# A four-layer residual kernel: the gated layer's first tokens and first weights prepared in the last two attention bodies, and output weights awaited where they are used

## What is computed

```python
x = x + L0(x)      # 16-head attention with coherence gate
x = x + L1(x)      # 16-head attention, masked, normalised output
h = rmsnorm(x) * g1 + b1
x = x + attention(h, Wq, Wk, Wv, Wo)                                        # L2, first half
h = rmsnorm(x) * g2 + b2
x = x + (silu(h @ gate_w.T) * (h @ hid_w.T)) @ out_w.T                      # L2, second half: the gated layer
x = x + mix(x)                                                              # L3, a 4x4 channel mix
```

## Time and profile before

| | |
|---|---|
| time, median of 3 runs | 3041.84 us (3039.84 to 3043.53) |
| profiled execution | 3037.38 us |
| its span, first to last instruction | 3035.6 us |
| PE busy | 2907.8 us, 96% of the span |
| DVE, ACT, POOL busy | 2051.9, 1363.4, 655.8 us |
| last attention matmul ends | 1914.05 us |
| first DMA of the gated layer is issued | 1918.83 us |
| first gate matmul of the gated layer starts | 1940.00 us |

### The profile page before, as it was taken

The page is one execution under the profiler, slowest core; times in us unless marked ns, Lnnn a source line. Parts: engine busy times, 40 slices in busy tenths (PEclk is TensorE's granted clock), DMA queues, the critical chain, the costliest instruction groups (busy, mean ns, idle before and its releaser), DMA issues. The chain is left out here.

```text
span 3035.6 us, 69785 instructions
## 1 busy us (share of the span) xinstructions
PE 2907.8 (96%) x27253; PEld 2524.4 (83%) x27253; DVE 2051.9 (68%) x3656; ACT 1363.4 (45%) x2222; POOL 655.8 (22%) x546
## 2 busy tenths in 40 slices
PE   5999999999899999998999999599999999999997
PEld 4899999998788999887888888488888888888886
DVE  5788778886688888887777777554444454655554
ACT  2555545554466666655566665322222232222221
POOL 0222222221121111132223332122222221111111
PEclk7999999999999999999999999699999999999999
DMA  3444444448444444574433344411111140111101
GB/s 137 90 127 123 131 125 124 128 116 193 128 100 102 109 100 102 128 178 119 111 104 111 100 108 99 159 56 56 56 63 62 65 157 29 42 56 42 55 28 42
DMA packets 515354, 300.45 MB, mean 99 GB/s; under 512 B 411776, under 2 KB 485632, under 8 KB 514720
## 3 DMA queue, kind: packets, MB, share of 16 engines
q1 hardware_dynamic: 515232, 298.76, 36.5%
HBM read 139.31 MB, written 58.72 MB: 65 GB/s over the span
## 5 line engine op out<-in xcount | busy, mean ns | idle before, releaser
L942 ACT ACTIVATE att_shifted<-att_shifted,keep_lift 128x512 f32<-128x512 f32 x384 | 276.1, 719 | 328.4 <-DVE att_shifted L1096 324.6
L1092 DVE TENSOR_REDUCE att_top<-att_bank_s 128x4 f32<-128x512 f32 x384 | 263.9, 687 | 203.6 <-PE att_bank_s L775 200.1
L1688 DVE TENSOR_TENSOR mlp_act_t<-mlp_bank_u,mlp_sg 128x512 f32<-128x512 f32 x128 | 88.4, 690 | 454.0 <-ACT mlp_sg L1590 450.4
L1730 POOL TENSOR_TENSOR mlp_al<-mlp_act_t,mlp_ah 128x512 fp32r<-128x512 f32 x128 | 174.7, 1365 | 857.0 <-ACT mlp_ah L1596 857.0
L1590 ACT ACTIVATE mlp_sg<-mlp_bank_g 128x512 f32<-128x512 f32 x128 | 76.5, 598 | 628.0 <-PE mlp_bank_u L1503 627.9
L937 ACT ACTIVATE att_pq<-att_shifted 128x512 f16<-128x512 f32 x384 | 240.7, 627 | 188.2 <-DMA att_pt<-att_pq 181.8
L1100 DVE TENSOR_TENSOR att_pq<-att_shifted,att_pq 128x512 f16<-128x512 f32 x384 | 266.9, 695 | 26.7 <-ACT att_pq L937 26.5
L1096 DVE TENSOR_TENSOR att_shifted<-att_bank_s,att_top 128x512 f32<-128x512 f32 x384 | 265.4, 691 | 16.3
L790 PEld LDWEIGHTS att_bank_o<-keep_v,att_pt 128*128 128x128 f16 x7680 | 213.1, 96 | 51.7 <-issue 15.6
L790 PE MATMUL att_bank_o<-keep_v,att_pt 128*128 128x34 bf16 x7680 | 237.8, 178 | 15.3 <-DMA att_pt<-att_pq 11.4
L726 PE MATMUL att_bank_a<-att_oth,att_woh 128*128 128x256 f32 x768 | 234.7, 306 | 1.5 <-DVE att_otl L1136 1.5
(11 more groups left out here) (254 smaller groups left out, 8121.4 us busy)
## 6 DMA issues: line engine op xcount, KB each, us to landing
resid<-att_xres SPq DMA_DIRECT2D x47, 512.0 KB, 2.8
mlp_xf<-resid SPq DMA_DIRECT2D x32, 512.0 KB, 5.0
mlp_res<-resid SPq DMA_DIRECT2D x32, 512.0 KB, 4.6
att_xin<-resid SPq DMA_DIRECT2D x31, 512.0 KB, 3.6
att_xres<-resid SPq DMA_DIRECT2D x31, 512.0 KB, 4.3
att_xin<-in_x SPq DMA_DIRECT2D x16, 512.0 KB, 4.5
att_xres<-in_x SPq DMA_DIRECT2D x16, 512.0 KB, 3.8
att_spare<-in_w_next SPq DMA_DIRECT2D x16, 512.0 KB, 3.9
```

The costliest lines, as they stand in the source:

```text
L942: nc.scalar.activation(shifted[:, u % 2], shifted[:, u % 2], ACT.Exp, bias=k["lift"][:, 0:1], scale=SCALE).then_inc(exp_done, 1)
L1092: nc.vector.reduce_max(top[:, u % 2, :], bank_s, AX_X).then_inc(top_ready, 1)
L1730: nc.gpsimd.tensor_tensor(al[:, c % 2, :], act_t[:, c % 2, :], f32(ah[:, c % 2, :]), ALU.subtract).then_inc(a_low, 1)
```

## The change

1. **Tiles that both phases share.** The attention weights of k and q now lie in one tile `w_gate` (high and low), those of v and o in `w_up`; the gated layer uses the same tiles as `wg` and `wu`. The tiles `hh`, `hl` (512 tokens wide) of the gated layer's first group are shared too: attention uses their first 256 columns as `xh`, `xl` in all its bodies. Room comes from one staging tile less in attention (`vr` stands in for it at the start).
2. **First tokens.** Bodies 46 and 47 run the same normalisation chain as the bodies before them, for groups "48" and "49", which are groups 0 and 1 of layer 2's own output, with gain and bias `g2`, `b2`. SP's loads of them stand at the end of bodies 45 and 46. Group 48 is split in body 47 into the left half of `hh`, `hl`; group 49 after body 47 into the right half.
3. **First weights.** At the end of body 46 SP loads gate and up weights of chunks 0 and 1 into the two spare tiles; ACT makes their high parts in slot 9 of body 47, DVE the low parts after body 47, between the last `low_output` and the last residual additions.
4. **The gated layer** starts without loads 0 and 1, without the first group's load, normalisation and splitting; `Splitter` counts from load 2 (`there=2`), loads 4 and 5 no longer wait for a staging tile, and PE's first two chunks wait for nothing but their banks. SP issues loads 2 to 5 first, then the six transfers of body 0 (tokens of group 1, residual, layer input).
5. **Output weights.** The wait of PE at the end of bodies 16 and 32 is gone; `project` waits for `new_weights["o", m]` at each output projection of layers 1 and 2. In body 16 SP issues the swap's last two loads before `store_piece`, not after it.

The core of the diff:

```diff
@@ Splitter
-            sp.wait_ge(self.low_done, self.before[n][-1] + 1)
+            sp.wait_ge(self.low_done, self.ready(self.before[n][-1]))
@@ attention
-        xh, xl = sb("xh", [P, CH, T], F32R), sb("xl", [P, CH, T], F32R)
+        xh, xl = hh[:, :, 0:T], hl[:, :, 0:T]
...
+        def has_x(i, ahead):
+            return has(i, ahead - 2)
...
         def pre(i):
-            return has(i, 2) and lay(i + 2) == 2
+            return has_x(i, 2) and lay(i + 2) == 2
...
+        def operands(n):
+            if isinstance(n, int) and n > ALL:
+                return hh[:, :, T:2 * T], hl[:, :, T:2 * T]
+            return xh, xl
@@ SP
-                    if u == 7 and has(i, 3) and lay(i + 3) == 2:
+                    if u == 7 and has_x(i, 3) and lay(i + 3) == 2:
                         load(i + 3)
                 if lay(i) != 1:
                     load_residual(i)
                 if post(i):
                     store(i - 1)
+                swap(i, UNITS)
+                if isinstance(i, int) and i == ALL - 2:
+                    for n, d in enumerate((a["gate_w"], a["hid_w"])):
+                        sp.dma_start(spare[n][:], d[:, 0:2].rearrange("p n c e -> p (n c e)")).then_inc(first_loaded[n], 16)
                 if piece_of(i) is not None:
                     store_piece(piece_of(i))
-                swap(i, UNITS)
@@ PE
                     if isinstance(p, int) and p > 0 and p % G == 0:
-                        for half in range(2) if kind == "v" else (m,):
+                        for half in range(2) if kind == "v" else (m,) if kind in "kq" else ():
                             pe.wait_ge(new_weights[kind, half], 32 * lay(p))
+                    if kind == "o" and lay(p) > 0:
+                        pe.wait_ge(new_weights["o", m], 32 * lay(p))
...
-                if isinstance(i, int) and i in (G, 2 * G):
-                    for m in range(2):
-                        pe.wait_ge(new_weights["o", m], 32 * lay(i))
@@ ACT
+            def first_weights_high():
+                for m, (kind, n) in enumerate((("k", ("k", 1)), ("v", ("v", 1)))):
+                    act.wait_ge(a_full[m], a_done(ALL - 1, n))
+                    act.wait_ge(first_loaded[m], 16)
+                    nc.scalar.activation(flat3(wh[kind][:, 0:2]), spare[m][:], ACT.Copy).then_inc(first_high, 1)
...
+                    if s == 9 and isinstance(i, int) and i == ALL - 1:
+                        first_weights_high()
             iterate(act, body)
             high_output(ALL - 1, 1)
+            high_x(ALL + 1)
@@ DVE
             low_output(ALL - 1, 1)
+            for m, kind in enumerate("kv"):
+                dve.wait_ge(first_high, m + 1)
+                nc.vector.tensor_tensor(flat3(wl[kind][:, 0:2]), spare[m][:], f32(flat3(wh[kind][:, 0:2])), ALU.subtract).then_inc(first_low, 1)
@@ POOL
             iterate(pool, body)
+            low_x(ALL + 1)
@@ gated_mlp, SP
-            move(0, x_in, xf, False, x_loaded)
-            for n in range(6):
+            for n in range(2, 6):
                 ws.load(sp, n)
@@ gated_mlp, ACT
-            squares(0)
-            deviation(0, 0, 1)
-            for n in range(2):
-                ws.high(act, n)
-            for e in range(CH):
-                high_h(0, e, 0)
             ws.high(act, 2)
@@ gated_mlp, DVE
-            add_squares(0)
-            norm_start(0)
-            for e in range(CH):
-                norm(0, e)
-                if e == 0:
-                    ws.low(dve, 0)
-            for n in range(1, 3):
-                ws.low(dve, n)
+            ws.low(dve, 2)
```

More of the change, by code:

```diff
@@ L77, with __init__ @@
 class Splitter:
[L79 to L82 removed]
+    def __init__(self, nc, hold, tag, loads, stage, there=0):
+        self.nc, self.loads, self.stage, self.there = nc, loads, stage, there
+        self.stage_of = [n % len(stage) for n in range(len(loads))]
+        self.before = [[m for m in range(there, n) if self.stage_of[m] == self.stage_of[n]] for n in range(len(loads))]
         self.loaded = [held(nc, hold, f"{tag}_w_loaded{n}") for n in range(len(stage))]
@@ L386, in attention @@
         cz, ce, cc, c8, cf = (sb(n, [P, NB * H]) for n in ("cz", "ce", "cc", "c8", "cf"))
-        spare = [sb(f"spare{n}", [P, CH // 2 * E]) for n in range(3)]
+        spare = [sb(f"spare{n}", [P, CH // 2 * E]) for n in range(2)]
         part_h, part_l = sb("part_h", [P, CH // 2 * E], F32R), sb("part_l", [P, CH // 2 * E], F32R)
@@ L403, in attention @@
                  for n in "cvo" for m, part in enumerate(halves)]
-        ws = Splitter(nc, hold, "att", loads, [t[:] for t in spare[:3]])
+        ws = Splitter(nc, hold, "att", loads, [spare[0][:], spare[1][:], vr[:].rearrange("p b e -> p (b e)")])
         PIECES = [(n, m) for n, m in (("k", 0), ("q", 0), ("v", 0), ("v", 1), ("k", 1), ("q", 1), ("o", 0), ("o", 1))]
@@ L617, in load @@
                     sp.wait_ge(x_split, n)
-                move(x_in[lay(n)], n, landing(n), False, x_loaded)
+                move(x_out[2] if beyond(n) else x_in[lay(n)], n, landing(n), False, x_loaded)
             def store(n):
@@ L1016, in body @@
                         nc.scalar.activation(root[:], eps[:], ACT.Sqrt)
-                    if s == 3 and has(i, 1):
+                    if s == 3 and has_x(i, 1):
                         high_x(i + 1)
@@ L1318, in body @@
                     third_values(i, b)
-                if has(i, 1) and lay(i + 1) != 1:
+                if has_x(i, 1) and lay(i + 1) != 1:
                     low_x(i + 1)
@@ L1361, in gated_mlp @@
         xf = sb("xf", [P, CH, FT])
[L1362 to L1363 removed]
+        hh, hl = [hh_first, sb("hh1", [P, CH, FT], F32R)], [hl_first, sb("hl1", [P, CH, FT], F32R)]
         res = sb("res", [P, CH, FT])
@@ L1766, in phase, with chunks @@
                 pass
-        def weight_tiles(wctx, tag, names):
-            return tuple({n: wctx.enter_context(nc.sbuf_tensor(f"{tag}_w{n}{part}", [P, CH, E], F32R)) for n in names} for part in "hl")
+        w_gate, w_up = ([keep(f"w{n}{part}", [P, 2, CH, E], F32R) for part in "hl"] for n in ("gate", "up"))
+        hh, hl = keep("hh", [P, CH, FT], F32R), keep("hl", [P, CH, FT], F32R)
+        wh, wl = ({n: t[:, at] for t, names in ((w_gate[part], "kq"), (w_up[part], "vo")) for at, n in enumerate(names)} for part in range(2))
+        def chunks(t):
+            return t[:].rearrange("p a c e -> p (a c e)").rearrange("p (n c e) -> p n c e", n=HC, c=CH)
         with ExitStack() as actx:
@@ L1782, in build @@
             phase(prepare, a, early)
-            phase(attention, [a["x"], scratch[0], scratch[1]], scratch[0:3], wh, wl, a, *split)
-        phase(gated_mlp, scratch[2], scratch[1], scratch[3], out, a["gate_w"], a["hid_w"], a["out_w"])
+            phase(attention, [a["x"], scratch[0], scratch[1]], scratch[0:3], wh, wl, a, *split, hh, hl)
+        phase(gated_mlp, scratch[2], scratch[1], scratch[3], out, a["gate_w"], a["hid_w"], a["out_w"], [chunks(t) for t in w_gate],
+              [chunks(t) for t in w_up], hh, hl)
 def kernel(**inputs):
```

104 lines of the change are left out of this document (45 added, 59 removed).

## The result

The changed kernel takes 2992.7 us (median of 4 runs, 2990.73 to 2994.78) against 3041.26 us for the kernel before (4 runs, 3039.84 to 3043.53): a ratio of 0.984, 95% interval 0.9823 to 0.9857. That is 48.6 us less; the forecast was 2997.3 us. Profile against profile, where the sum was made, the span fell from 3035.6 to 2989.9 us, 45.7 us, against 44.5 in the sum. (`span` is the time from the first to the last instruction of the profiled execution.)

The account below looks back on a forecast made before the run. PE, busy 96%, bounds the kernel through its matmuls, gaps and half-clock stretches. 8.4 + 11.2 + 26.0 − 1.1 = 44.5 us off the median 3041.84 gives 2997.3 us, range 2990.0 to 3009.0.

Parts of the forecast that it names:

- Stall 1: End of body 16: removing PE's output-weight wait of 6.37 us and the half clock behind it saves 8.4 us.
- the clock's 2.0 us: After body 16's wait: PE's next loop round runs at half clock, costing 2.0 us that goes with the wait.
- Stall 2: End of body 32: removing the 8.82 us output-weight wait and 2.4 us of half clock saves 11.2 us.
- The slack: Output weights land before the second projection needs them, 7.4 us early in body 17, 4.8 in body 33; no added wait.
- The gated layer, −26.0: Gated layer's first DMA issue (T0) to the root of the next group's squares: 44.2 us becomes 18.2, saving 26.0.
- PE's own 13.3 us: Gated layer's start: PE's first two chunks, with some 2.4 us of half clock, take 13.3 us from T0.
- The tail: Attention's last bodies: added work costs 1.1 us, 0.2 in body 46 and 0.9 in body 47; bounds −1.4 and +9.3.
- A: Gated layer: loads 2 to 5 share DMA with six transfers, load 5 up to 9.0 us later; gain 35.5; chance 0.10.
- B: Output weights: half clock stays and body 33 waits 4.8 us again; gain 35.3, 3006.5 us; chance 0.08.
- C: Body 47: all 9.3 us of its new work show instead of 0.9; gain 36.1, 3005.7 us; chance 0.07.
- E: Phases' border: something still holds PE some 11 us; gain 33.5, 3008.3 us; chance 0.05.
- D: All attention bodies: matmuls reading half of wider shared rows cost 10 ns more each, 3066.4 us; chance 0.02.

Follow-up runs that it names:

- the weights alone: Changed kernel with the first tokens loaded and normalised in the gated layer again, only the first weights prepared early: 3016.79 us, ratio 0.9921.
- the order of loads: Changed kernel with SP issuing the six transfers of body 0 first and loads 2 to 5 behind them: 3003.43 us, ratio 0.9883.
- the kernel without the border's wait: Changed kernel, attention's last store awaited only in the gated layer, with splits, squares and loads reordered: 2988.48 us; again 2993.44 beside the changed kernel's 2995.36.
- the first tokens alone: Changed kernel with weight loads 0 and 1 loaded and split in the gated layer again, only first tokens prepared early: 3001.55 us, ratio 0.9865.

## Why the prediction was right

The measured 2992.7 lies in the range of 2990.0 to 3009.0, 4.6 below the point; the median moved 48.6 for 44.5 forecast, the span 45.7. Most of the 4.6, 3.6 us, is not in any step: the forecast took the medians of both kernels to lie 4.5 us above their profiled executions, and the changed kernel's lies 0.9 above. Step by step:

- **Stall 1, −8.4.** The wait's part held: no kernel in which each projection waits for its own half waits for output weights. Of the clock's 2.0 us the first profile shows 1.4. PE at the end of body 16 and entering 17, in the changed kernel (stretch, busy PE, PEld, DVE, ACT, POOL, granted clock, DMA share, GB/s):

```profile
778.00:783.00 5.00, 4.92 (x46) 3.79 (x47) 1.31 (x4) 1.69 (x2) 0.00 (x0) 0.66 1.04 343
783.00:788.00 5.00, 5.00 (x53) 4.81 (x52) 2.13 (x4) 3.44 (x7) 2.20 (x2) 1.00 0.35 138
```

  The clock is at half there for a while still, behind a wait of 1.58 us for a transpose at the body's end. Over all pairings of the table 7.1 to 8.8 us came, 7.8 in the first profile.
- **Stall 2, −11.2.** 11.0 in the first profile, but 8.1 to 11.1 over all pairings of the table: the first profile has the top end, and the term was a little high.
- **The slack.** Right. In the first profile the last load leaves 2.5 us before its use in body 33, not 4.8; counted to the start of that projection, 2.3 here, it is 2.3 to 6.5 over the eleven profiles, with 4.8 inside. Counted from the first scores behind the old wait's place (1369.44), it landed after 10.8 us, before after 8.8 (1377.74 to 1386.56), and the projection was reached after 13.1, not 13.7.
- **The gated layer, −26.0.** 25.6. Issue order, split and table load stand; load 5 landed at T0 + 8.9 for 8.3 (the first later than the sum had it, the rest 1.3 us apart, not 1.5). PE's own 13.3 us were 14.1 in this profile and 13.3 to 14.1 in the six: over two chunks at full clock, 10.9 us, that is 2.4 to 3.1 us of half clock, where the sum had 2.4. An estimate by the page "ScalarE: Activation LUTs" of the Trainium skill, section "What ACT_TABLE_LOAD costs", had the silu start 2.66 us behind the load's start. It was 1.30, and the measurement decides.
- **The tail, +1.1.** +0.2 from two errors that nearly cancel, which is luck: body 45 gave 1.4 back, which I had kept as a bound and set to 0, and body 47 up to T0 cost 1.5 in this profile, not 0.9. In the second profile of the same kernel it cost 0.4. The chain's own cost shows in the distance from the body's first maximum to its last: 20.11 and 20.95 us in the kernels without part 2's edits, 20.81 with the weights alone, and 21.11 to 21.99 in the eight with the chain where the change has it. What tells the two profiles apart is PE's clock, which the prediction left out here. In the second half of body 47 PE is idle for much of the time (busy 7.5 of 13 us in the first row below), and its clock is at half for some 17 us, in the kernel before too. The first two rows are of the changed kernel's first profile, the third of its second. The second and the third cover the same part of the body, 36 to 39 us behind its first maximum (columns as above):

```profile
1875.28:1888.28 13.00, 7.48 (x100) 6.45 (x101) 9.90 (x14) 7.14 (x9) 5.14 (x9) 0.50 0.43 88
1888.28:1891.28 3.00, 3.00 (x16) 3.00 (x16) 1.82 (x1) 0.00 (x0) 0.74 (x1) 0.50 0.00 0
```
```profile
1892.98:1895.98 3.00, 3.00 (x25) 3.00 (x25) 2.64 (x2) 0.00 (x0) 0.86 (x1) 0.89 0.00 0
```

  The clock came back 39.3 us behind the first maximum in the first profile and 36.7 in the second, in the middle of the last output projection, and T0 came 1.1 us later in the first.
- **Rivals.** A (shared DMA) fell by the order of loads; B (the wait returns) by eleven traces without it; C (no room in body 47) by body 47's 0.4 to 1.5 us in place of 9.3; E (something holds the start) did not come: what holds PE there is the border's wait of 4.8 us, which both kernels have. D (the shared tile is dearer) fell with the bodies of all layers: 41.80 us each in the loop of layer 0 with the shared tile, 41.83 without, 34.41 to 34.47 for 34.47 to 34.49 in layer 2. No matmul pays for the wider rows.
- **What lay outside the sum.** 2.9 us gained ahead of body 16 and 2.1 lost in bodies 18 to 31 nearly cancel in the first profile. Both lie within the scatter of the 14 profiles; that the timing of transfers makes it is likely, and not shown. A sum over one profile can't have it.

## What to carry to other kernels

A wait belongs in front of the instruction that reads, not at the loop's door: 15 us of waiting and 1 to 4 us more, most of it half clock, went by that, with no other work moved. Where one phase must prepare operands before PE can start, prepare the first of them under the last bodies of the phase before; but take the longest chain first, for here the tokens brought 19.8 us alone and the weights at most 0.9. When two paths to a start are within a microsecond of each other, one profile can't say what an edit to either is worth: here the same code scattered by 1.5 us.

## What the runs showed of the hardware

- PE's clock could fall after the engine had resumed. In the kernel without the border's wait PE paused for 2.62 us and then ran (stretch and columns as above):

```profile
1896.90:1898.30 1.40, 1.36 (x6) 1.18 (x7) 0.06 (x1) 0.00 (x0) 0.00 (x0) 1.00 0.35 132
1898.30:1901.00 2.70, 2.70 (x9) 2.10 (x8) 0.00 (x0) 0.00 (x0) 0.00 (x0) 0.52 0.68 192
```

  So PE ran at half clock for 3.4 us after the shorter pause, in both profiles of that kernel, and for 4.6 to 6.1 us after the pause of 4.85: the stretch came later and was shorter, but it did not go.
- The same subtraction on DVE, 128x1024, took 1.22 us, and 3.40 when POOL began a subtraction of the same size just before it, which took 2.43; in the kernel without the border's wait DVE began first, and there it took 1.22 and POOL's 3.44. With the first tokens alone POOL had it to itself and took 2.37. So whichever began first took its usual time, and the other ended as if it had waited for that. In the changed kernel, DVE and POOL:

```profile
1885.56 1.22 DVE L1302 TENSOR_TENSOR keep_wgatel<-att_spare,keep_wgateh 128x1024 fp32r<-128x1024 f32 x1
1886.69 3.40 DVE L1302 TENSOR_TENSOR keep_wupl<-att_spare,keep_wuph 128x1024 fp32r<-128x1024 f32 x1
```
```profile
1886.59 2.43 POOL L1311 TENSOR_TENSOR keep_hl<-att_xf,keep_hh 128x1024 fp32r<-128x1024 f32 x1 [1.17 <-ACT keep_hh L1008]
```

  Both lie under the output projection here and cost nothing; on a path of waits the 2.2 us would have.
